# Moving every SBUF tensor that TensorE reads to a chosen place in a 512-byte period

## The reference

```python
q = jnp.einsum('bchw,dc->bdhw', x, theta_w) + theta_b[None, :, None, None]      # d = 256
xpool = _maxpool2(x)                                                           # 16 x 16
k = jnp.einsum('bchw,dc->bdhw', xpool, phi_w) + phi_b[None, :, None, None]
v = jnp.einsum('bchw,dc->bdhw', xpool, g_w) + g_b[None, :, None, None]
qk = jnp.einsum('bdn,bdm->bnm', q, k) * hp ** (-0.5)                            # 1024 x 256
p = jax.nn.softmax(qk, axis=-1)
vp = jnp.einsum('bdm,bnm->bdn', v, p)
out = jnp.einsum('bdhw,cd->bchw', vp, z_w) + z_b[None, :, None, None]
return out + x
```

## The kernel before, in words

| family | function | stationary | moving | columns | matmuls |
|---|---|---|---|---|---|
| q | `project_q` | `theta` | `x_split` | 512 | 3072 |
| K | `project_k` | `phi` | `xp` | 256 | 1536 |
| V | `project_v` | `xp` | `g` | 256 | 1536 |
| scores | `scores` | `q` | `k` | 256 | 1536 |
| attention | `attend` | `vt` | `pt` | 512 | 768 |
| output products | `project_out` | `z` | `att` | 256 | 5376 |

## Time and profile before

### The profile page before, as it was taken

One profiled execution on the slowest core, in us unless ns is written; L12 is line 12 of the kernel. 1 busy time (PEld: TensorE's weight loads), 2 busy tenths in 40 slices (PEclk: granted clock), 3 DMA queues, 4 the chain that ended last, 5 costly groups with the idle time before them and its releaser, 6 DMA issues.

```text
span 2110.6 us, 41060 instructions
## 1 busy us (share of the span) xinstructions
PE 2070.1 (98%) x13824; PEld 1889.0 (90%) x13824; DVE 1563.4 (74%) x2619; ACT 1294.4 (61%) x2228; POOL 1374.1 (65%) x833
## 2 busy tenths in 40 slices
PE   7899999999999999999999999999999999999996
PEld 6799999999999999999999999999999999999995
DVE  8786776876777877767867778767778677677665
ACT  5566565665666665666655656656666656566553
POOL 4676666776666766666766667766677666677643
PEclk9999999999999999999999999999999999999998
DMA  6556556556466555566565665555664655655635
GB/s 219 176 179 208 170 204 219 194 184 206 165 211 232 170 202 177 188 219 211 177 209 169 199 228 176 201 189 174 214 227 167 207 170 203 219 194 184 203 102 174
DMA packets 212903, 407.21 MB, mean 193 GB/s; under 512 B 12688, under 2 KB 15760, under 8 KB 212880
## 3 DMA queue, kind: packets, MB, share of 16 engines
q1 hardware_dynamic: 212736, 406.90, 57.5%
q10 hardware_dynamic: 144, 0.01, 0.0%
HBM read 272.64 MB, written 134.22 MB: 193 GB/s over the span
## 4 chain that ended last, share of the span: by engine, by line
PE 94%; DVE 3%; POOL 1%; DMA 1%; issue 1%; ACT 1%; SPq 0%; DVEq 0%; ACTq 0%
PE bank L797 94%; DVE pt_raw L631 1%; DMA x<-x 1%; DVE x_top L649 0%; DVE x_bot L649 0%; POOL pt_lo L528 0%; DVE g_lo L595 0%; POOL att_f L531 0%; DVE x_split_lo L680 0%; ACT probs L430 0%; DVE pooled L603 0%; DVE att_f L662 0%; DVE q_lo L609 0%; POOL att_lo L536 0%; POOL x_split_lo L518 0%
## 5 line engine op out<-in xcount | busy, mean ns | idle before, releaser
L518 POOL TENSOR_TENSOR x_split_lo<-x,x_split_hi 128x1024 fp32r<-128x1024 f32 x254 | 612.8, 2419 | 268.9 <-ACT x_split_hi L333 264.1
L797 PE MATMUL bank<-att_hi,z_hi 128*128 128x256 f32 x1792 | 498.3, 278 | 15.5 <-POOL att_lo L536 6.2
L797 PE MATMUL bank<-att_lo,z_hi 128*128 128x256 f32 x1792 | 497.3, 278 | 0.0
L797 PE MATMUL bank<-att_hi,z_lo 128*128 128x256 f32 x1792 | 497.2, 277 | 0.0
L631 DVE STREAM_TRANSPOSE pt_raw<-probs 32x256 f32<-32x256 f32 x1024 | 445.9, 435 | 18.1 <-ACT probs L430 1.5
L797 PE MATMUL bank<-x_split_hi,theta_hi 128*128 128x512 f32 x1024 | 407.8, 398 | 11.0 <-POOL x_split_lo L518 9.8
L797 PE MATMUL bank<-x_split_lo,theta_hi 128*128 128x512 f32 x1024 | 404.7, 395 | 0.0
L797 PE MATMUL bank<-x_split_hi,theta_lo 128*128 128x512 f32 x1024 | 403.8, 394 | 0.0
L649 DVE TENSOR_TENSOR x_top<-bank,x_top 128x512 f32<-128x512 f32 x512 | 334.7, 688 | 86.3 <-PE bank L797 79.4
L536 POOL TENSOR_TENSOR att_lo<-att_f,att_hi 128x512 fp32r<-128x512 f32 (+1 forms) x192 | 283.1, 1480 | 173.0 <-ACT att_hi L372 173.0
L333 ACT ACTIVATE x_split_hi<-x 128x1024 fp32r<-128x1024 f32 x256 | 271.1, 1059 | 155.1 <-PE bank L797 149.6
(11 more groups left out here) (67 smaller groups left out, 4072.4 us busy)
## 6 DMA issues: line engine op xcount, KB each, us to landing
x<-x SPq DMA_DIRECT2D x256, 512.0 KB, 3.9
x_top<-x SPq DMA_DIRECT2D x128, 512.0 KB, 7.0
x_bot<-x SPq DMA_DIRECT2D x128, 512.0 KB, 5.2
out<-x_top SPq DMA_DIRECT2D x128, 512.0 KB, 3.6
out<-x_bot SPq DMA_DIRECT2D x128, 512.0 KB, 6.7
x_top<-theta_wt SPq DMA_DIRECT2D x4, 256.0 KB, 6.2
x_top<-g_wt SPq DMA_DIRECT2D x4, 256.0 KB, 7.0
x_bot<-z_wt SPq DMA_DIRECT2D x4, 256.0 KB, 6.9
```

Of the source, the lines that this page charges most:

```text
L518: nc.gpsimd.tensor_tensor(flat(lo), flat(x_chunk(s, c)), raw(flat(hi)), ALU.subtract).then_inc(x_ready, 1)
L797: last = nc.tensor.matmul(dst, stationary(a), moving(b), start=start and n == 0, stop=stop and n == len(PRODUCTS) - 1, skip_group_check=re ...
```

## The change

Nothing is computed differently and no instruction is added, removed or reordered. The SBUF tensors are allocated in another order, and four unused tensors of 64 bytes (`pad_z`, `pad_g`, `pad_rows`, `pad_phi`) stand between groups of them.

```diff
-        theta = [sb(f"theta_{s}", [P, KT, D], f32r) for s in ("hi", "lo")]
...
         bias = sb("bias", [P, NB], f32)
         phi_bias = sb("phi_bias", [P, DT], f32)
...
         negmax = sb("negmax", [P, NT], f32)
         rowsum = sb("rowsum", [P, NT], f32)
         rowinv = sb("rowinv", [P, NT], f32)
+
+        xp = [sb(f"xp_{s}", [P, KT, M], f32r) for s in ("hi", "lo")]
+        k = [sb(f"k_{s}", [P, DT, M], f32r) for s in ("hi", "lo")]
+        att = [sb(f"att_{s}", [P, 7, HB], f32r) for s in ("hi", "lo")]
+
+        sb("pad_z", [P, 16], f32)
+        zw = [sb(f"z_{s}", [P, 7, TB * P], f32r) for s in ("hi", "lo")]
+
+        sb("pad_g", [P, 16], f32)
+        gw = [sb(f"g_{s}", [P, KT, D], f32r) for s in ("hi", "lo")]
+
+        sb("pad_rows", [P, 16], f32)
+        q = [sb(f"q_{s}", [P, DT, H], f32r) for s in ("hi", "lo")]
+        theta = [sb(f"theta_{s}", [P, KT, D], f32r) for s in ("hi", "lo")]
+        xs = [[sb(f"x_split_{s}{i}", [P, KC, H], f32r) for s in ("hi", "lo")] for i in range(XS)]
+        vt = [sb(f"vt_{s}", [P, MT, D], f32r) for s in ("hi", "lo")]
+        pt = [sb(f"pt_{s}", [P, MT, H], f32r) for s in ("hi", "lo")]
+
+        sb("pad_phi", [P, 16], f32)
+        phi = [sb(f"phi_{s}", [P, KT, D], f32r) for s in ("hi", "lo")]
+        weights = [theta, phi, gw]
+
+        xb = [sb(f"x{i}", [P, KC, H], f32) for i in range(XB)]
+        x_top = [sb(f"x_top{i}", [P, TB, H], f32) for i in range(2)]
...
```

More of the change, by code:

```diff
@@ L89, in sem @@
             return ctx.enter_context(nc.semaphore(name))
-        theta = [sb(f"theta_{s}", [P, KT, D], f32r) for s in ("hi", "lo")]
[L93 to L96, removed]
         bias = sb("bias", [P, NB], f32)
         phi_bias = sb("phi_bias", [P, DT], f32)
+        negmax = sb("negmax", [P, NT], f32)
+        rowsum = sb("rowsum", [P, NT], f32)
+        rowinv = sb("rowinv", [P, NT], f32)
+        xp = [sb(f"xp_{s}", [P, KT, M], f32r) for s in ("hi", "lo")]
[14 more added lines that the diff above has]
+        weights = [theta, phi, gw]
         xb = [sb(f"x{i}", [P, KC, H], f32) for i in range(XB)]
-        xs = [[sb(f"x_split_{s}{i}", [P, KC, H], f32r) for s in ("hi", "lo")] for i in range(XS)]
         x_top = [sb(f"x_top{i}", [P, TB, H], f32) for i in range(2)]
@@ L107, in non_local_block @@
         pooled = sb("pooled", [P, KT, MH], f32)
[L108 to L111, removed]
         probs = sb("probs", [P, NT, M], f32)
-        negmax = sb("negmax", [P, NT], f32)
-        rowsum = sb("rowsum", [P, NT], f32)
-        rowinv = sb("rowinv", [P, NT], f32)
         pt_raw = sb("pt_raw", [P, MT, H], f32)
-        pt = [sb(f"pt_{s}", [P, MT, H], f32r) for s in ("hi", "lo")]
         att_f = sb("att_f", [P, 8, HB], f32)
-        att = [sb(f"att_{s}", [P, 7, HB], f32r) for s in ("hi", "lo")]
         bank = [ctx.enter_context(nc.psum_tensor(f"bank{i}", [P, 512], f32)) for i in range(8)]
```

## The result

The kernel after takes 2117.60 us (median of 11 runs, 2116.37 to 2119.87) against 2112.09 us for the kernel before on the same chips: ratio 1.0027, interval 1.0019 to 1.0035. It is 5.5 us slower, where I had predicted 49 us faster. The time lies inside the range I gave, the sign is the wrong one.

A forecast was written before the change was run, and what follows sets the result against it. TensorE's matmul count times start distance was taken as the bound. K, scores and V 25.5 plus q and attention 25.7 gave 51.2 us, 49 after the 96% share: 2112.4 - 49 = 2063 us, range 2030 to 2120.

The forecast's parts named there:

- What bounds the kernel: TensorE's unbroken matmuls: time is their number times the distance between starts, 2053 us of a span of 2110.6.
- Sorted by place ... The only family with both operands on whole lines is the only fast one: 256-column matmuls: output, on whole lines, took 113.3 ns; scores, K and V took 117.3 to 119.6.
- The hint from the last V matmul: Last V matmul, loading `theta` on whole lines: 0.11 us before q's first, against V's own 0.117; called weak.
- K, scores, V at 113.3, 25.5 us: These 256-column families, moved to whole lines, were to reach the output's 113.3 ns and gain 25.5 us.
- q and attention at 226.6, 25.7 us: These 512-column families, moved to place 0 on whole lines, were to take twice the output's distance and gain 25.7 us.
- the middle one of my three values: For q and attention: 226.6 ns, gaining 25.7 us, between 219.8 ns (51.8 us gained) and nothing gained.
- The output products ... I take no change: Output matmuls go from place 3 to 7 on whole lines: no change, bounds 36.6 us gained and 33.9 us lost.
- Rival D: Output products leave a good place, 3, for 7 and slow down: 2148 us, or 2135 us with the tail's 117.8; chance 0.17.
- a D that is partly paid back: Upper end of the range, 2120 us: 8 us above no change, for an output loss partly offset by gains.
- Rival C: Places do nothing; the families differ through PSUM or the order of products: 2112 us, chance 0.08.
- The other engines' tiles at nothing: Tiles of VectorE, ScalarE, GpSimd and DMAs move too, costed at nothing; closest cover `att_lo` with 1.7 us of slack.

The follow-up runs named there:

- cross_05: Against the kernel after: all 256-column families at place 3, q and attention at 0, `x_split` minus `z` 0.5 lines; 2084.18 us, ratio 0.9867.
- after_half: The kernel after with every large tensor 32 bytes further, so every operand begins on a half line; 2117.75 us, ratio 1.0028.
- after_entry: The kernel after with `z` and `att` both half a line further, so `x_split` minus `z` goes from 2 to 1.5 lines; 2101.82 us, ratio 0.9949.
- the two before_entry kernels: The kernel before with `z` and `att` half a line lower or higher, `x_split` minus `z` 2 or 1 instead of 1.5; 2134.19 and 2132.22 us.
- v_jump: cross_05 with `xp`, `phi` and `g` half a line lower, K and V still at place 3; 2085.44 us, ratio 0.9874.
- cross_10: cross_05's layout with `theta`, `x_split`, `vt` and `pt` moved so that `x_split` minus `z` is 1 line; 2097.84 us, ratio 0.9932.
- before_q0: The kernel before with q and attention alone at place 0, all their operands on half lines; 2102.49 us, ratio 0.9955.
- after_o3: The kernel after with the output products back at place 3, by moving `z` and `att`; 2117.57 us, ratio 1.0027.
- before_o7: The kernel before with the output products alone at place 7, by moving `z`; 2112.16 us, ratio 1.0000.
- after_q15: The kernel after with q and attention back at place 1.5 (`theta` and `vt` at line 6.5); 2124.81 us, ratio 1.0058.
- before_entry_1: The kernel before with `z` and `att` half a line higher, so `x_split` minus `z` is 1 line instead of 1.5; 2132.22 us, ratio 1.0096.

## Why the prediction was wrong

*What bounds the kernel*, the distances, and that a change in them counts in full: right. The long piece of the chain took up the difference between the medians, 5.46 of 5.5 us in the kernel after and 28.0 of 27.9 in cross_05.

*"Sorted by place ... The only family with both operands on whole lines is the only fast one"*: this reading failed, and it is the step on which K, scores and V rested. after_half has every operand on half lines and is the same as after. The output was fast with a jump of 1.5 from q; after_entry and the two before_entry kernels show its rhythm go with that jump at an unchanged place. I had made a rule of lines out of one family in six, and had noted the tail's 117.8 ns, which contradicts it, only in a rival. The hint from the last V matmul, 0.11 us, says nothing: V's own distances in that row go from 0.11 to 0.12 us.

*K, scores, V at 113.3, 25.5 us*: measured 120.0, 117.9 and 118.8, which in sum gains nothing (+0.5, -2.6, +2.3 us). That 256-column families can run at 113.3 was right: K does in cross_05, and the scores there and V in v_jump once they have settled. The change didn't put them there.

*q and attention at 226.6, 25.7 us*: 226.7 is what they settle to (cross_10 has it in whole rows), so the middle one of my three values was the right size. But each row of 12 spends its first matmuls settling, and q's last one, with `z` being loaded, takes 233 ns again, which leaves 228.5 and 228.4: 3840 x 4.9 = 19 us. In before_q0, with other jumps, the same place gains 9.6 us. So the size of this term was overestimated by what a row spends at its two ends; and what it was argued from, whole lines, is not what brings it, as after_half and before_q0 have it on half lines.

*"The output products ... I take no change"*: here the sign was lost, 24 us. This term was put at nothing because the output stayed on whole lines. Rival D had the size of it (23 us with the tail's 117.8 for the output) and the wrong mechanism: it held that place 3 gives the fast rhythm and 7 does not, and after_o3 and before_o7 show the two alike. What decided is the jump from q, 1.5 to 2. The change altered jumps without aiming at them. D's price was meant with no gain elsewhere; the real case is D's loss beside the gain of q and attention, 24 - 19, which falls between my cases, near no change. That the time lies inside the stated range is owed to its upper end, which allowed for "a D that is partly paid back", and not to any case that I had worked out.

*Rival C* was nearly right in its time for the wrong reason: places and jumps do a lot, they cancelled. (What I held against it, "three different distances", was misread: scores and K both have 119.6.) Its rule of the Trainium skill ("SBUF — State Buffer", section "Who interferes with whom": TensorE's two read ports are independent, "PE and ACT never wait on anyone") does not cover what the runs show: 2084 to 2134 us by where the tensors lie, with TensorE's waits on other engines the same within 5 us, and 15.8 us between after and after_entry, which differ by 32 bytes in `z` and `att`.

*The other engines' tiles at nothing*: right. Their tiles moved in every reordered kernel, and the waits of TensorE stayed as they were (32 to 37 us in all).

What is open: why there are two rhythms, and what it is in the state of a family that its successor takes over. The jump that I moved changes two things at once, which line of `z` is loaded during the last q matmul, and where `att` starts after `x_split`; no run separates them. That weight load and moving stream meet in SBUF would fit the dependence on differences of addresses; it is not shown by any run on its own. The exceptions (after_q15, the rows of 12 in before_entry_1, V behind fast and slow scores) show that place and jump together don't fix the rhythm. For the output no place other than 3 and 7 was tried.

## What to carry to other kernels

Where matmuls follow each other without a break, read the distance between starts, per family, and not the busy time: here 113.3 or 117.8 ns for the same matmul is 24 us in 2112. Where the operands lie relative to each other moves it, and not only within a family: how a family is entered can pick a rhythm that then lasts for the row. Steps of 32 bytes counted; 256 bytes more or less for `z` changed nothing. So operands can't be placed family by family; measure the whole order, and after each move look at the families that were not moved.

## What was not expected of the hardware

- Rows settle to a repeating pattern with one of a few means: 113.3, 117.8 or 120.0 ns for 256 columns (V also 117.3 and 118.8) and 226.7 or 233.3 ns for 512. The single distances can be even (113, 113, 114) or far apart (q in the kernel before: 231, 237, 232). 113.3, 120.0, 226.7 and 233.3 are 17, 18, 34 and 35 times 6.67 ns. At half clock a column takes 426 / 512 = 0.83 ns, so 6.67 ns is 16 columns at 2.4 GHz, or 64 bytes of fp32; that this is more than a coincidence is not shown.
- The same matmul at the same addresses and full clock runs at either 113.3 or 117.8 ns in one execution (kernel before: middle and tail; kernel after: tail and middle).
- At half clock the loss does not show: 426 ns for 512 columns in the kernel before, half of which is 213 against the 226.7 to 233.3 at full clock.
- The times go from 2084.18 to 2134.19 us, 2.4%, by nothing but the order and the padding of SBUF tensors.
